# The projection's waits by bank, its modulated columns written twice by ScalarE, and a shorter lead of attention's maxima

## What is computed

```python
h = _layernorm(x, axis=-1) * (1 + ca) + sa
x = x + ga * _L0_attn_ref(h, ...)
# in _L0_attn_ref
Q = lora_linear(x, Wq, bq, Aq, Bq).reshape(bsz, seq_len, NUM_HEADS, HEAD_DIM)
K = lora_linear(x, Wk, bk, Ak, Bk).reshape(bsz, seq_len, NUM_HEADS, HEAD_DIM)
V = lora_linear(x, Wv, bv, Av, Bv).reshape(bsz, seq_len, NUM_HEADS, HEAD_DIM)
scores = jnp.einsum('bqhd,bkhd->bhqk', Q, K) / np.sqrt(HEAD_DIM).astype(np.float32)
```

## Time and profile before

| what | value |
| --- | --- |
| median of 3 runs | 5367.38 us (5358.28 to 5378.68) |
| the profiled execution's own time | 5363.83 us |
| span of its trace | 5362.3 us |
| TensorE busy | 4843.6 us (90%) |
| VectorE busy | 4327.3 us (81%) |
| ScalarE busy | 3148.3 us (59%) |
| GpSimd busy | 1495.1 us (28%) |

### The profile page before, as it was taken

The page is one execution under the profiler, slowest core; times in us unless marked ns, Lnnn a source line. Parts: engine busy times, 40 slices in busy tenths (PEclk is TensorE's granted clock), DMA queues, the critical chain, the costliest instruction groups (busy, mean ns, idle before and its releaser), DMA issues. The chain is left out here.

```text
span 5362.3 us, 106154 instructions
## 1 busy us (share of the span) xinstructions
PE 4843.6 (90%) x34561; PEld 2570.9 (48%) x34561; DVE 4327.3 (81%) x6781; ACT 3148.3 (59%) x5713; POOL 1495.1 (28%) x1082
## 2 busy tenths in 40 slices
PE   5849999999999999999999599996999999856998
PEld 3723333333333333333333377774656565544666
DVE  4768999999999999999999578876988888872000
ACT  1307888888888888888888223232455445432111
POOL 1311111111111111111111233333666666643233
PEclk7959999999999999999999799997999989857999
DMA  4842222222222222222212211112000000044442
GB/s 134 285 106 49 51 44 41 42 45 49 54 42 42 46 41 49 54 42 45 45 38 51 66 48 35 47 35 62 19 20 22 22 18 20 27 159 141 145 154 98
DMA packets 236412, 339.97 MB, mean 63 GB/s; under 512 B 60119, under 2 KB 169938, under 8 KB 227132
## 3 DMA queue, kind: packets, MB, share of 16 engines
q1 hardware_dynamic: 219744, 275.39, 21.4%
q0 software_dynamic: 16192, 58.43, 3.1%
HBM read 205.62 MB, written 136.18 MB: 64 GB/s over the span
## 5 line engine op out<-in xcount | busy, mean ns | idle before, releaser
L694 DVE TENSOR_REDUCE at_mxp<-at_ps_m 128x2 f32<-128x1024 f32 x2098 | 2531.9, 1221 | 90.8 <-PE at_ps_m L747 68.3
L667 ACT ACTIVATE at_prob<-at_ps_s 128x512 f32<-128x512 f32 x4100 | 2227.4, 596 | 326.6 <-PE at_ps_s L737 299.0
L757 PE MATMUL at_ps_o<-at_prob,at_vs 128*32 128x256 f32 x16384 | 1312.7, 392 | 19.6 <-ACT at_osum L673 13.9
L737 PE MATMUL at_ps_s<-at_qs,at_ks 51*128 51x512 f32 x4100 | 1036.8, 501 | 1.8 <-ACT at_prob L667 1.8
L747 PE MATMUL at_ps_m<-at_ks,at_qs 49*128 49x512 f32 x4196 | 863.7, 407 | 67.4 <-DMA at_ks<-t_parts 50.0
L737 PEld LDWEIGHTS at_ps_s<-at_qs,at_ks 51*128 51x128 f32 x4100 | 385.0, 183 | 850.3 <-ACT at_prob L667 850.2
L757 PEld LDWEIGHTS at_ps_o<-at_prob,at_vs 128*32 128x32 f32 x16384 | 323.9, 108 | 783.8 <-ACT at_prob L667 396.0
L564 POOL TENSOR_TENSOR at_total<-at_total,at_minus 128x16 f32<-128x16 f32 x65 | 189.6, 2917 | 1611.7 <-DMA at_total<-at_osum 1611.7
L747 PEld LDWEIGHTS at_ps_m<-at_ks,at_qs 49*128 49x128 f32 x4196 | 405.2, 190 | 93.5 <-DMA at_ks<-t_parts 50.4
L2306 ACT ACTIVATE ex_hid<-ex_ps_h,ex_b 128x512 f32<-128x512 f32 x128 | 87.9, 687 | 388.4 <-PE ex_ps_h L2322 388.4
L1497 DVE SCALAR_TENSOR_TENSOR sc_cv<-sc_xc,sc_conv_w,sc_cv 128x512 f32<-128x512 f32 x255 | 264.9, 1070 | 20.6 <-issue 7.0
(11 more groups left out here) (304 smaller groups left out, 6168.2 us busy)
## 6 DMA issues: line engine op xcount, KB each, us to landing
t_parts<-pr_parts SPq DMA_DIRECT2D x64, 512.0 KB, 4.9
ex_w<-in_fw SPq DMA_DIRECT2D x32, 1024.0 KB, 7.5
at_qs<-t_parts SPq DMA_DIRECT2D x102, 256.0 KB
at_ks<-t_parts SPq DMA_DIRECT2D x102, 256.0 KB
t_buf<-at_blank POOLq DMA_DIRECT2D x64, 384.5 KB, 3.8
at_vs<-t_v SPq DMA_DIRECT2D x17, 1024.0 KB, 4.8
ex_rest<-t_buf SPq DMA_DIRECT2D x16, 1026.0 KB, 5.1
t_v<-pr_vaug SPq DMA_DIRECT2D x64, 256.0 KB, 4.7
```

Of the source, the lines that this page charges most:

```text
L667: nc.scalar.activation(prob[0 if up is None else (t + 1) % 2][:, j, :], ps_s[bank][:, :], ACT.Exp).then_inc(s_read, 1)
L694: nc.vector.tensor_reduce(out[:, s4, k + i, 2 * pair:2 * pair + 2], ps_m[i][:, :, :], AX.X, ALU.max).then_inc(mx_read, 1)
L737: nc.tensor.matmul(ps_s[bank][:, :], ks[s][a:a + QROWS, j // 2, t1 * P:(t1 + 1) * P], qs[s][a:a + QROWS, j // 2, c * T:(c + 1) * T], start ...
L757: last = nc.tensor.matmul(ps_o[32 * j:32 * j + 32, q0:q1], vs[s][:, t, 32 * j:32 * j + 32], prob[t % 2][:, j, q0:q1], start=(t == 0 and ha ...
```

## The change

Four things change. TensorE's wait ahead of a group's product asks for that group's own second part of the chunk before, and `low_done` starts at G so that the count is positive. ScalarE writes the modulated columns twice, once rounded into the upper part and once in full, and raises `hT_done` for each of the two blocks. VectorE makes the lower part, in two subtractions behind the normalisation; the cast on VectorE and the subtraction on GpSimd go. `LEAD` is 22 tiles where it was 25, so `NEXT` is 10 where it was 7.

```diff
-                            sp.wait_ge(low_done, i * G + g + 1)
+                            sp.wait_ge(low_done, (i + 1) * G + g + 1)
...
-                def lower_rows(n, h):
-                    pool.wait_ge(upper_done, n + 1)
-                    lower_part(nc.gpsimd, hTc[h][1][:, :, :], hT[h][:, :, :], hTc[h][0][:, :, :]).then_inc(hT_cut, 1)
...
-                def upper_rows(n, h):
+                def lower_rows(n, h):
 
-                    dve.wait_ge(hT_done, n + 1)
-                    upper_part(nc.vector, hTc[h][0][:, :, :], hT[h][:, :, :]).then_inc(upper_done, 1)
+                    for k in range(KD):
+                        dve.wait_ge(hT_done, KD * n + k + 1)
+                        last = lower_part(nc.vector, hTc[h][1][:, k, :], hT[h][:, k, :], hTc[h][0][:, k, :])
+                    last.then_inc(hT_cut, 1)
...
+                dve.sem_inc(low_done, G)
                 variance(0, 0, 0)
...
-                upper_rows(0, 0)
+                lower_rows(0, 0)
...
                         variance(i + 2, b * 2 + (c + 2) // 2, c % 2)
-                        upper_rows(i + 1, (c + 1) % 2)
                         second_part(i, 0)
                         normalise(i + 2, c % 2)
+                        lower_rows(i + 1, (c + 1) % 2)
                         second_part(i, 1)
...
                     for k in range(KD):
-                        last = nc.scalar.activation(hT[h][:, k, :], ps_t[k][:, :], ACT.Identity,
-                                                    scale=mcur[:, k:k + 1], bias=mcur[:, KD + k:KD + k + 1])
-                    last.then_inc(hT_done, 1)
+                        for out in (hTc[h][0], hT[h]):
+                            last = nc.scalar.activation(out[:, k, :], ps_t[k][:, :], ACT.Identity,
+                                                        scale=mcur[:, k:k + 1], bias=mcur[:, KD + k:KD + k + 1])
+                        last.then_inc(hT_done, 1)
...
-                    pe.wait_ge(hT_done, n)
+                    pe.wait_ge(hT_done, KD * n)
...
-                    pe.wait_ge(low_done, i * G)
+                    pe.wait_ge(low_done, i * G + g + 1)
...
-        LEAD = TILES + 9
+        LEAD = TILES + 6
```

More of the change, by code:

```diff
@@ L270, in project_phase @@
         tr_done, hT_done, qk_done, qk_out = sem("tr_done"), sem("hT_done"), sem("qk_done"), sem("qk_out")
-        w_cut, upper_done, hT_cut = sem("w_cut"), sem("upper_done"), sem("hT_cut")
+        w_cut, hT_cut = sem("w_cut"), sem("hT_cut")
         low_done, slopes_in, slopes_cut, slopes_stored = sem("low_done"), sem("slopes_in"), sem("slopes_cut"), sem("slopes_stored")
@@ L329, in _ @@
                     load(n + 2, n)
-                lower_rows(0, 0)
                 with loop(nc, pool, 0, B) as b:
@@ L334, in _ @@
                         rsqrt(i + 2)
-                        lower_rows(i + 1, (c + 1) % 2)
                         wait_alone(pool, xh_done, i + 3, always)
```

## The result

The changed kernel takes 5313.88 us (median of 4 runs, 5298.21 to 5325.90) against 5370.24 us before (4 runs, 5358.28 to 5378.68); the ratio is 0.990 with a 95% interval of 0.988 to 0.992. The forecast was 5313. The traces show that single terms missed by up to 9 us, in opposite directions, so the closeness is partly luck. The profiled execution took 5311.8 us (span 5310.3), 52.0 us less than the one before.

The account below looks back on a forecast made before the run. The projection was taken as a ring of waits with no engine full, attention's loop as filled by TensorE. Gains 26.4 + 6.7 + 0.8 + 6.8 + 13.65 = 54.4 us off 5363.83 give 5309.5, plus 3.55: 5313 us, range 5300 to 5322.

Parts of the forecast that it names:

- the wait by bank: Projection's fourteen steady chunks: waiting only for the same bank's second part brings 12.79 us a chunk to 10.9, gaining 26.4 us.
- the case: Projection, sign of a DMA bound: a share near 1 all through and ScalarE waiting for stores.
- the DMA term: Projection: DMA engines need 11.25 us a chunk at a share of 1, about 10.7 at 1.05.
- near tie: Projection: TensorE (9.5 to 10.8 us a chunk) and DMA (about 10.7) nearly tie, so 10.9 was taken.
- the tail: Projection's last chunk: wins 0.8 us since VectorE is faster; the drain of the stores behind it stays.
- the clock's part: Projection: TensorE takes 9.54 us a chunk at the high clock, 10.80 at the mix; TensorE-alone rival at 9.6, 5295 us, chance 0.08.
- the sentence that the wait alone was the lock: Projection: the wait for all four second parts causes 2.0 us of idleness a chunk; by bank, no cause is left.
- start: Projection's first chunk: VectorE subtracts right behind the slopes, first product near 79 us, second chunk's at 93.0, not 99.70; gain 6.7.
- lead-in: Before attention's loop: LEAD 22 in place of 25 saves six VectorE reductions of 1.13 us each, 6.8 us.
- The 358 GB/s: Projection: the skill's HBM rate allows no chunk below 10.25 us; 9 us less, 5304, about 2 in 10 of the forecast's range.
- block 0: Attention's first block: moved band loads end ScalarE's stall, 53.65 us to 40.0, gain 13.65; rival, stall stays, 5327 us, chance 0.27.
- the deadline: Attention loop: row of maxima still lands before TensorE's last-tile wait, by 1.8 to 2.5 us; rival, late row, chance 0.04.

Follow-up runs that it names:

- The moved cut: Kernel before with only double write on ScalarE and subtraction on VectorE, waits as before, LEAD 25: 5333.40 us, ratio 0.994.
- the value rows: Changed kernel with the value buffer laid out by group, so stores move 2 KB pieces in place of 512 B: 5296.40 us, ratio 0.987.
- the experiment that moves only the load: Changed kernel with LEAD 25 and the second band's load moved from the end of block 0 to block 1: 5317.80 us, ratio 0.991.

## Why the prediction was right, and where it was not

**Right: the wait by bank and what takes its place.** The 2 us of idleness ahead of the first product went, and the DMA engines became the bound of the projection, with a share of 1.04 and ScalarE waiting for stores, as the case was put. Chunks came 10.21 us apart, though, not 10.9. The step that missed is the size of the DMA term. I took 11.25 us of the engines' time a chunk as fixed, divided by the share 1.05 of one microsecond, got 10.7, and added 0.2 for a near tie. The share was nearly right, 1.04 over 143 us. But a chunk took only 1.04 x 10.21 = 10.6 us of the engines' time. Some 0.35 us of the difference are bytes that moved later: 348 GB/s x 10.21 us is 3.55 MB a chunk and not 3.67. The rest stays unexplained. The missing 0.12 MB a chunk, 1.6 MB over the fourteen, turn up in the tail, where 7.4 MB passed and not 5.9, and at 348 GB/s they are 4.6 us. The tail was 4.6 us worse than forecast: I gave it a gain of 0.8, and it lost 3.8. That the bytes moved there the traces show; that they are what the tail waited for is worked out, not tried. Steady chunks and tail together gained 31.5 us, forecast 27.2.

**Not seen: the clock's part.** TensorE's clock was in the forecast only as a range, 9.5 to 10.8 us. In every kernel whose idle gap shrank the mean grant of the steady chunks was 0.99 or 1.00, so about 1.0 us of the 12.73 a chunk was clock, not work. No run changes the gap alone, so that the gap is what lowered the clock is likely and not shown. The moved cut was costed as a help to VectorE that changes no period. Alone it gains 1.6 us a chunk with the old wait in place, so it is a second way round the same limit, and the sentence that the wait alone was the lock fell.

**Right: start and lead-in.** The first product came at 77.36 us (forecast 78.9; 1.2 us of the difference is earlier work), the second chunk 8.6 us earlier (6.7). Normalisation is faster with GpSimd's subtraction gone, 409 ns a quarter chunk in place of 770, so 1.64 us a chunk where I had 1.38. With the waits changed alone, and the subtraction still on GpSimd, it took 777. The groups by line, of the kernel before and of the changed one, with the columns of the earlier trace rows:

```profile
L361 DVE TENSOR_SCALAR pr_xh<-pr_xin,pr_mv,pr_rstd 128x256 f32<-128x256 f32 x72 | 51.1, 770 | 2.3 <-POOL pr_rstd L318 2.3
```

```profile
L355 DVE TENSOR_SCALAR pr_xh<-pr_xin,pr_mv,pr_rstd 128x256 f32<-128x256 f32 x72 | 24.8, 409 | 5.5 <-POOL pr_rstd L318 5.5
```

The two rows agree with the rule that the prediction quotes from the Trainium skill (SBUF — State Buffer, section "SBUF: two separate sides"). For a VectorE operation with two SBUF inputs that page limits its rule to a GpSimd operation that reads SBUF; the two new subtractions took 688 ns each, against 692 for the same form, so nothing held them up.

The lead-in lost 6.8 us, as forecast. The 358 GB/s of the Trainium skill (SBUF — State Buffer, section "A bandwidth-pool intuition that's wrong (but worth ruling out)") would have given 10.25 us a chunk, near the 10.21 measured, but for a reason that the value rows refute.

**Half right: block 0.** The long idleness went, from 5.9 to 1.5 us, and the experiment that moves only the load shows that the load stretched it. But I booked the whole 13.65 us, as if the block could run at 40.0 us: I took all of its low grant to be the stall's consequence, and the stall to go altogether. In the kernel before, the block opened with 9 us at the low grant, ahead of the stall:

```profile
398.73:407.73 9.00, 9.00 (x50) 3.01 (x51) 4.77 (x4) 4.84 (x10) 2.93 (x1) 0.52 0.04 5
```

In the changed kernel it opened with 15. Block 0 gained 5.9 us; of the 7.8 that are missing, 6.3 are this opening stretch and 1.3 the rest of the stall. Between kernels the stretch lasted from 9 to some 21 us, which goes along with no edit that I can name, and stays open. By the estimate above that is worth about 5 us, so it can be only a small part of the 28 us between the runs of the changed kernel.

**Right: the deadline.** It held, with 4 us of slack and not 2. The row lands in 1.4 us where I allowed 2 to 2.8, and from the negation to the end of the last issue it takes 6.1 us (1024.69 to 1030.83) where I counted the 6.9 of the earlier trace rows. The cliff is where it was put: 64 blocks times the lateness, seen at LEAD 20.

**How the sum was met.** Against the forecast the steady chunks gave 8.9 us more, the start 1.9 and the loads of attention 0.6; block 0 gave 7.8 less, the tail 4.6 and all behind it 1.3. That is 11.4 more and 13.7 less: the profiled time fell by 52.0 us where 54.4 were forecast. The median of the runs lies 2.1 us above the profiled 5311.8, where I had added 3.55. So 5313 against 5313.88 is partly luck: single terms were off by up to 9 us, and the part behind block 0, which spreads over some 21 us, happened to lie 1.3 us from the one before.

## What to carry to other kernels

When a ring of waits has a gap, list all ways to close it before adding their gains: here a finer wait and a shorter neighbour gave 32 and 34 us by the medians, and 40 together, since the next bound stood just behind. A DMA share near 1 doesn't prove that the DMA engines are the bound; waits for their transfers, and a run with fewer bytes or longer pieces, do. Add to such a bound what it still owes at the stage's end. A lead can be cut as far as its deadline's slack, which is measured by cutting too far once: below it, every block pays.

## What the runs showed of the hardware

TensorE's granted clock stayed at 1.00 with 1.56 us of idleness in every 11.1 us (the moved cut alone), and averaged 0.90 with 2.0 us, at most 2.6, in every 12.7 (the kernel before). The lower clock cost about 1.0 us a chunk, an estimate from one chunk at the full grant; that the few tenths of a microsecond of idleness made the difference is likely and not shown.

At one instruction of attention's first block ScalarE stood idle in all twelve profiles with nothing to wait for: 4.1 to 5.9 us in the four in which a load of 1 MB had been issued 1 to 5 us before, and 1.4 to 2.2 us in the other eight.

Value stores in pieces of 2 KB in place of 512 B, with the same bytes, raised what the DMA engines held over 130 us from 348 to 371 GB/s. The share of the DMA engines was 1.01 and 0.99 in two kernels in which ScalarE never waited for a store, and 1.04 where it did.
